# An fp32 attention product as three fp32r products, and the token mix shared between ScalarE and VectorE

## What is computed

```python
mod = (silu(c) @ wmod).reshape(8, 6, 1, -1)
sa, ca, ga, sb, cb, gb = (mod[:, n] for n in range(6))
ga = sign(ga) * maximum(abs(ga), 0.25)         # gb the same
h = layernorm(x) * (1 + ca) + sa
x = x + ga * attn(h)
h = layernorm(x) * (1 + cb) + sb
x = x + gb * ffn(h)

def attn(x):                       # 8 heads of 64; softmax over features, not tokens
    q, k, v = split(x @ w_qkv + b_qkv)
    scores = einsum('bhld,bhle->bhde', q, k) / sqrt(64)
    out = einsum('bhld,bhde->bhle', v, softmax(scores))
    return layernorm(out @ w_fc + b_fc + x) * gamma + beta

def ffn(x):
    prev = x shifted by one token (zeros first)
    xr = mu_r * x + (1 - mu_r) * prev
    xk = mu_k * x + (1 - mu_k) * prev
    r = sigmoid(xr @ W_r.T); k = xk @ W_k.T
    return r * (square(relu(k)) @ W_v.T)
```

## Time and profile before

| what | value |
|---|---|
| median of 3 runs | 691.06 us (689.15 to 691.09) |
| profiled execution, its own time | 690.6 us |
| its span, first to last instruction | 688.9 us |
| mean granted TensorE clock | 0.991 |
| TensorE matmuls, busy | 670.7 us, 97% |
| VectorE, busy | 561.0 us, 81% |
| ScalarE, busy | 393.8 us, 57% |
| GpSimd, busy | 317.5 us, 46% |

### The profile page before, as it was taken

The page is one execution under the profiler, slowest core; times in us unless marked ns, Lnnn a source line. Parts: engine busy times, 40 slices in busy tenths (PEclk is TensorE's granted clock), DMA queues, the critical chain, the costliest instruction groups (busy, mean ns, idle before and its releaser), DMA issues.

```text
span 688.9 us, 11754 instructions
## 1 busy us (share of the span) xinstructions
PE 670.7 (97%) x3712; PEld 539.4 (78%) x3712; DVE 561.0 (81%) x1254; ACT 393.8 (57%) x871; POOL 317.5 (46%) x520
## 2 busy tenths in 40 slices
PE   7988999999999999999999999999999999999896
PEld 6777886888778887879868887788878788687674
DVE  5693999789887998889887898979988898658973
ACT  1424575566754675474855667546754747547662
POOL 5272864573254642565335742646325753214320
PEclk9989999999999999999999999999999999999999
DMA  8849345485836666572855849366665528628225
GB/s 316 232 152 222 103 131 123 77 212 97 209 74 142 163 135 147 99 167 92 198 113 79 219 91 213 67 141 158 145 136 99 107 72 173 123 37 179 37 31 91
DMA packets 90984, 93.02 MB, mean 135 GB/s; under 512 B 4224, under 2 KB 89000, under 8 KB 90960
## 3 DMA queue, kind: packets, MB, share of 16 engines
q0 software_dynamic: 33264, 33.03, 32.6%
q1 hardware_dynamic: 55344, 55.97, 25.6%
q10 hardware_dynamic: 2352, 3.73, 1.5%
HBM read 42.84 MB, written 33.10 MB: 110 GB/s over the span
## 4 chain that ended last, share of the span: by engine, by line
PE 86%; DVE 7%; POOL 2%; DMA 2%; issue 1%; ACT 1%; SPq 0%; DVEq 0%; POOLq 0%
PE work L1335 14%; PE work L1318 14%; PE att L1285 13%; PE gram L1267 11%; PE gram L1398 4%; PE att L1370 4%; PE work L1151 4%; PE tr L1260 4%; PE work L1153 4%; PE work L1152 4%; PE tr L1302 4%; PE att L1389 2%; PE gram L1380 1%; PE att L1318 1%; DVE st L907 1%
## 5 line engine op out<-in xcount | busy, mean ns | idle before, releaser
L471 POOL TENSOR_TENSOR rs<-ve,neg_half 128x4 f32<-128x4 f32 x32 | 41.6, 1300 | 161.4 <-DVE ve L917 161.4
L1285 PE MATMUL att<-m_sb,z_t 128*128 128x256 f32 x496 | 112.4, 380 | 1.6 <-issue 0.8
L1335 PE MATMUL work<-mx,w_k_t 128*128 128x512 f32 x236 | 106.2, 592 | 0.0
L1285 PEld LDWEIGHTS att<-m_sb,z_t 128*128 128x128 f32 x496 | 92.4, 190 | 16.9 <-issue 5.7
L1318 PE MATMUL work<-w_r_t,mx 128*128 128x256 f32 x464 | 105.7, 381 | 0.0
L1318 PEld LDWEIGHTS work<-w_r_t,mx 128*128 128x128 f32 x464 | 85.9, 190 | 11.1
L1267 PE MATMUL gram<-z 128*128 128x256 f32 (+1 forms) x512 | 90.7, 331 | 0.0
L1267 PEld LDWEIGHTS gram<-z 128*128 128x128 f32 x512 | 81.1, 194 | 6.9
L934 DVE SCALAR_TENSOR_TENSOR mx<-t_buf,mu_col,h2t 128x512 f32<-128x512 f32 x120 | 84.3, 765 | 1.1
L654 ACT ACTIVATE sq<-att 128x256 f32<-128x256 f32 x124 | 46.1, 383 | 64.1 <-PE att L1285 64.1
L1335 PEld LDWEIGHTS work<-mx,w_k_t 128*128 128x128 f32 x236 | 44.8, 190 | 44.1 <-issue 42.6
(11 more groups left out here) (170 smaller groups left out, 1283.6 us busy)
## 6 DMA issues: line engine op xcount, KB each, us to landing
x_in<-in_L_attn_x_dram SPq DMA_DIRECT2D x32, 512.0 KB, 4.8
x<-rows SPq DMA_DIRECT2D x32, 512.0 KB, 3.4
x<-in_L_attn_x_dram POOLq DMA_DIRECT2D x32, 512.0 KB, 8.9
out_dram<-x SPq DMA_DIRECT2D x31, 512.0 KB, 5.1
out_dram<-y POOLq DMA_DIRECT2D x29, 512.0 KB, 6.2
rows<-row_scratch SPq DMA_DIRECT2D x16, 128.0 KB, 4.1
rows<-row_scratch SPq DMA_DIRECT2D x8, 256.0 KB, 3.8
wqkv_sb<-in_L_attn_w_qkv_dram ACTq DMA_DIRECT2D x1, 1536.0 KB, 9.7
```

The source lines that it names most:

```text
L1285: ins = mm(att_banks(j, alone)[q][:, (t % 2) * D:(t % 2 + 1) * D], z_t[:, j, k, t * P:(t + 1) * P], m_sb[:, k], start=(k == 0), stop=(k == ...
L1335: ins = mm(k_banks(alone)[dh][:], w_k_t[:, ch, rows_dh], mixed(j, alone)[1][:, ch], start=(ch == 0), stop=(ch == KD - 1))
```

## The change

Four things change together.

1. The attention product uses the same three-product form as the feed-forward output: z_t is replaced by z_hi (ScalarE's copy now rounds to fp32r) and z_lo (VectorE subtracts, low_z), and M by m_hi and m_lo (VectorE, two more instructions in make_m). The banks tr are free only when z_lo is made.
2. The mix of rows 0 to 6 has no difference any more. ScalarE writes mu times h2 (scale_r, scale_k: four activations per chunk), and VectorE adds (1 - mu) times the shifted h2 (mix_r, mix_k: four multiply-adds). The last row keeps the old form (mix_alone), but with the ordinary buffers.
3. k_hi and k_lo have one buffer in place of two; the last chunk of all uses z_hi.
4. Lists in another order, mostly around chunks 1 and 3; GpSimd's prep_wv stands later in the row; in the start, VectorE makes z_lo of row 0 and the column 1 - mu (make_rest), and ScalarE waits for the small loads.

```diff
@@ attention, TensorE
-                            ins = mm(att_banks(j, alone)[q][:, (t % 2) * D:(t % 2 + 1) * D], z_t[:, j, k, t * P:(t + 1) * P], m_sb[:, k],
-                                     start=(k == 0), stop=(k == KD - 1))
+                            ins = mm3(att_banks(j, alone)[q][:, (t % 2) * D:(t % 2 + 1) * D],
+                                      (z_hi[:, j, k, tile], z_lo[:, j, k, tile], m_hi[:, k], m_lo[:, k]),
+                                      start=(k == 0), stop=(k == KD - 1))
@@ turn_z2, TensorE
-                elif not last and j < CH - 1:
-                    pe.wait_ge(z_t_ready, 2 * (i + 1 + CH) + 2)
+                    if not last and j < CH - 1:
+                        pe.wait_ge(z_lo_ready, 2 * (i + 1 + CH) + 1 + h)
@@ ScalarE
+            def scale_r(b, j):
+                i = CH * b + j
+                wait_past(act, r_done, 2 * i - 2)
+                act.wait_ge(h2_ready, 2 * i + 2)
+                for h in range(KD):
+                    nc.scalar.activation(mixed(j)[0][:, h], h2t[:, h, 1 + j * CT:1 + (j + 1) * CT], ACT.Copy,
+                                         scale=mu_col[:, 0, h:h + 1]).then_inc(xr_scaled, 1)
...
@@ VectorE
+            def mix_r(b, j):
+                i, dst = CH * b + j, mixed(j)[0]
+                dve.wait_ge(xr_scaled, 2 * i + 2)
+                for h in range(KD):
+                    ins = nc.vector.scalar_tensor_tensor(dst[:, h], h2t[:, h, j * CT:(j + 1) * CT], rest_col[:, 0, h:h + 1],
+                                                         dst[:, h], ALU.mult, ALU.add)
+                ins.then_inc(xr_mixed, 1)
...
+            def low_z(b, j):
+                i = CH * b + j
+                for h in range(KD):
+                    dve.wait_ge(z_hi_ready, 2 * i + h + 1)
+                    nc.vector.tensor_tensor(z_lo[:, j, h], tr[h][:], z_hi[:, j, h].bitcast(F32),
+                                            ALU.subtract).then_inc(z_lo_ready, 1)
@@ make_m, VectorE
-                                        res[:].rearrange("p k d -> p (k d)"), ALU.add).then_inc(m_ready, 1)
+                                        res[:].rearrange("p k d -> p (k d)"), ALU.add).then_inc(m_step, 1)
+                dve.wait_ge(m_step, 2 * b + 1)
+                nc.vector.tensor_copy(m_hi[:], m_sb[:]).then_inc(m_step, 1)
+                dve.wait_ge(m_step, 2 * b + 2)
+                nc.vector.tensor_tensor(m_lo[:], m_sb[:], m_hi[:].bitcast(F32), ALU.subtract).then_inc(m_ready, 1)
@@ row_steps, ScalarE
                 copy_h2(b, 1)
+                make_z2(b, 2)
+                scale_r(b, 1)
+                copy_z_hi(n, 3)
                 squares(b, 3)
-                make_z2(b, 2)
-                copy_z_t(n, 3)
+                scale_k(b, 1)
                 copy_gram(n)
@@ start, VectorE
+            low_z(0, 2)
             rows_b()
+            low_z(0, 3)
             centre_fc()
+            make_rest()
             stats_a(1, 0)
```

More of the change, by code:

```diff
@@ L152, in adaln_block @@
         xr, xk = mx[:, 0], mx[:, 1]
-        k_hi, k_lo = (part(n, [P, 2, KD, CT]) for n in ("k_hi", "k_lo"))
+        k_hi, k_lo = (part(n, [P, KD, CT]) for n in ("k_hi", "k_lo"))
         y = sb("y", [P, 2, NT, D])
@@ L529, in row_steps @@
                 else:
-                    prep_wv(n)
                     rstd_o(b, 1)
@@ L917, in stats_2, with make_rest, mix_k, mix_alone @@
                 nc.vector.tensor_scalar(ve_2[:, s], ag_2[:, s, :, 1], EPS_LN, None, ALU.add).then_inc(ve_2_done, 1)
-            def mix(b, j, made=None, alone=False):
-                i = CH * b + j
[L922 to L927, removed]
+            def make_rest():
+                dve.wait_ge(small_loaded, 16 * 5)
+                nc.vector.tensor_scalar(rest_col[:], mu_col[:], -1.0, 1.0, ALU.mult, ALU.add).then_inc(rest_ready, 1)
+            def mix_r(b, j):
[5 more added lines that the diff above has]
+                ins.then_inc(xr_mixed, 1)
+            def mix_k(b, j):
+                i, dst = CH * b + j, mixed(j)[1]
+                dve.wait_ge(xk_scaled, 2 * i + 2)
+                for h in range(KD):
+                    ins = nc.vector.scalar_tensor_tensor(dst[:, h], h2t[:, h, j * CT:(j + 1) * CT], rest_col[:, 1, h:h + 1],
+                                                         dst[:, h], ALU.mult, ALU.add)
+                ins.then_inc(xk_mixed, 1)
+            def mix_alone(b, j, made):
+                i = CH * b + j
+                dve.wait_ge(r_done, 2 * i - 2)
+                dve.wait_ge(k_done, 2 * i - 2)
+                dve.wait_ge(xk_mixed, i)
+                dve.wait_ge(x2_ready, CH * b + made)
                 dve.wait_ge(h2_ready, 2 * i + 2)
@@ L930, in mix @@
                 nc.vector.tensor_tensor(dif, h2t[:, :, 1 + j * CT:1 + (j + 1) * CT], prev, ALU.subtract).then_inc(dif_done, 1)
-                dve.wait_ge(dif_done, i + 1)
-                for n, (dst, ready) in enumerate(zip(mixed(j, alone), (xr_mixed, xk_mixed))):
+                dve.wait_ge(dif_done, j + 1)
+                for n, (dst, ready) in enumerate(zip(mixed(j), (xr_mixed, xk_mixed))):
                     for h in range(KD):
@@ L1033, in row_steps @@
                 prep_now(n)
+                low_z(n, 0)
                 make_x2(b, 0)
@@ L1042, in row_steps @@
                 else:
+                    make_z(n, 2)
+                    low_k(b - 1, 3)
                     prep_qk(n)
-                    low_k(b - 1, 3)
-                    make_z(n, 2)
+                    low_z(n, 1)
                     make_x2(b, 1)
                     stats_2(b, 1)
-                mix(b, 0)
+                mix_r(b, 0)
+                mix_k(b, 0)
+                low_z(n, 2)
                 if first:
@@ L1057, in row_steps @@
                 make_z(n, 3)
-                mix(b, 1)
+                mix_r(b, 1)
+                low_z(n, 3)
                 gate_o(b, 0)
+                mix_k(b, 1)
                 make_x2(b, 3)
-                mix(b, 2)
+                mix_r(b, 2)
+                mix_k(b, 2)
                 low_k(b, 1)
@@ L1116, in _ @@
             make_z(0, 1, first=True)
+            low_z(0, 0)
             stats_a(0, 3)
@@ L1120, in _ @@
             prep_now(0)
+            low_z(0, 1)
             make_z(0, 3, first=True)
```

105 lines of the change are left out of this document (65 added, 40 removed).

## The result

The changed kernel takes 692.25 us (median of 15 runs, 690.96 to 695.2); the kernel before took 690.64 in the 15 runs beside it (688.79 to 692.7). The ratio is 1.0028, 95% interval 1.0015 to 1.0041: if anything slower, by 0.3%, which is less than the 2.1 us that the prediction took for the least that counts. Forecast were 680.6 and a range of 674 to 688, so the gain of 10 us did not come. The profiled execution took 692.31, with a span of 690.6 (before 690.6 and 688.9).

The account below looks back on a forecast made before the run. The prediction took TensorE's own work to bound the steady rows. Six steady rows at -13.7, row 0 +5.0 and last row -1.5 gave -10.2 from 690.6; time put at 680.6 us, 8-in-10 range 674 to 688.

Parts of the forecast that it names:

- part 4: GpSimd's moved wv step: make_z regains 2.5 us, the mix of chunk 2 loses 2.1, hidden by 2.6 of room.
- The third rival: Full block by GpSimd: mix of chunk 2 stopped 5.1 us, k_lo of chunk 1 2.5 late; 695.4 us, chance 0.06.
- the three signs of being wrong: Period above 78.6 or below 77.4; largest new steady-row TensorE wait elsewhere than forecast; row 0 under 3 us later.
- Part 1: Attention product on TensorE: 2.74 us instead of 3.45, saving 0.71 per chunk, 2.84 per row.
- Part 3: ScalarE's four scalings per chunk at 0.62 us each make TensorE wait 0.55 per row for the Gram copy.
- Part 2: VectorE's low z parts and M split, less the mix's difference: net +1.1 us per row, no steady-row cost from the split.
- The start and row 0: VectorE leads: 0.9 at the start, 1.15 for the M split, 2.4 added work, 0.55 Gram wait; 5.0 us later.
- The last stretch: Last row: no low_z but shorter attention products, half of the 2.84 let through, -1.5 us.

Follow-up runs that it names:

- b1: The kernel before with one edit, GpSimd's prep_wv moved to its new place, row 0 included: 703.59 us, ratio 1.0192.
- a2: The changed kernel with ScalarE's k scaling of chunk 1 moved behind the Gram copies: 730.27 us, ratio 1.0565.
- b2: The changed kernel with, in the loop's rows, prep_wv at its old place and VectorE's prep_qk behind make_z of chunk 3: 684.06 us, ratio 0.9897.
- c2: b2 with all three products of the attention product made from the high parts of z and M: 683.7 us, ratio 0.9896.
- b3: b2 with Gram copies ahead of chunk 3's squares and r of chunk 1 ahead of chunk 2's k scaling, row 0 too: 691.44 us, ratio 1.0014.
- c3: b2 with, in the loop's rows, Gram copies ahead of chunk 1's k scaling and r of chunk 1 ahead of chunk 2's: 684.9 us, ratio 0.9918.
- a1: The changed kernel with prep_wv back at its old place in the loop's rows: 690.53 us, ratio 0.9994.
- a4: The changed kernel with the edit of a2 and prep_wv one step earlier, where VectorE makes z of chunk 3: 706.35 us, ratio 1.0216.
- a3: The changed kernel with the edits of a1 and a2 together: 699.07 us, ratio 1.0112.
- b4: The changed kernel with its attention product in plain fp32, low part of z made but not used: 706.12 us, ratio 1.0207.
- c1: b2 with SyncE no longer waiting for M's low part before loading the next ca row: 683.51 us, ratio 0.9890.

## Why the prediction was wrong

**The step that failed is part 4, the sentence "between it and the k_lo of chunk 1 I count 2.6 us of room, so nothing shows".** The count of room was about right. The loss was not: I took 2.1 from row 0, and it is 4.25. Output 1 begins 2.0 late, so the room was 2.25 and not 2.6, and with the 0.32 that comes back in the product 1.68 per row is left. That is 10 us over six rows, most of the miss of 11.65. The trace of before held the answer. The mix of row 0, 95.81 to 100.65, met the first of GpSimd's two products, 97.40 to 100.10, and ended 0.55 after it; the second ran all but its first 0.47 beside VectorE instructions that read PSUM, which lost nothing. GpSimd's row, then VectorE's:

```profile
100.18 2.22 POOL L499 TENSOR_TENSOR wv_aug<-wv_aug 128x1020 f32<-128x1020 f32 x1
```

```profile
100.58 1.27 DVE L952 SCALAR_TENSOR_TENSOR y<-y,work 128x512 f32<-128x512 f32 x2
101.77 1.65 DVE L896 SCALAR_TENSOR_TENSOR t_buf<-att,rs_o,g_row 128x256 f32<-128x256 f32 x4
```

At the new place each of the two products meets a VectorE instruction with both inputs in SBUF. I read one meeting as the price of the step, when it was the price of one instruction. The third rival had the mechanism, at 0.06; its own price (5.1 lost, 2.5 late) was too high by 0.85 in the loss and 0.5 in the lateness, and what was blocked was the residual sum and half of the mix, not the mix alone. Two of the three signs of being wrong that the prediction names came: the period is above 78.6, and the largest new wait is not ScalarE's but the one before output 1.

b1 shows this piece alone, a2 shows the block at full length (7.00 for 1.41, one instruction held by each product), and b2 shows that with the meeting taken out of both places in the loop rows the kernel is 1.0% faster than before.

**Part 1.** The products save, but about 0.59 each, not 0.71: three of the four in a row take 2.86 to 2.96 from start to start and not the output product's 2.74. Four make -2.35 with their neighbours, not -2.84; 2.9 us over six rows. The row that I took for the price was the same form in another place, and c2 shows that the low parts are not the reason for the difference. Read from start to start, that same output product took 2.93 in the kernel before (288.61 to 291.54 in TensorE's timeline), so part of the 0.71 was in the reading.

**Part 3** was right: scalings of 0.62, no gap, a wait of 0.66 at the Gram transpose against 0.55. Another order of ScalarE's list, which I did not claim to help, didn't in b3 and c3.

**Part 2.** The M split costs nothing in a steady row; k_lo of chunk 0 and the turn of z2 hold. What I missed is that the new VectorE list leaves prep_wv's old place without cover as well (a1).

**The start and row 0.** Together +4.0 against +5.0, a near hit that is partly luck: the early part was taken too high, and 1.1 of row 0 comes from a wait that was not forecast. The start has +0 and not +0.9. From the mark to the output product of chunk 0, row 0 is 2.5 later (42.49 after the mark, before 39.99) and not 1.15 + 2.4 = 3.55, for the ca row came only 0.3 later after the mark (10.67 against 10.35), not 1.15. Then come the Gram transpose (+0.5) and output 1 (+1.1, with 0.91 of idle time), the block again.

**The last stretch.** -1.0 against -1.5.

With the two mis-sized terms put right my sum reads 680.6 + 10.0 + 2.9 = 693.5 against 692.25.

## What to carry to other kernels

When a GpSimd step is moved, price it instruction by instruction: for each of its large products, find which VectorE instruction on SBUF operands will stand beside it, and count that one as starting anew when GpSimd's ends. A slowed pair of rows seen elsewhere in the trace gives the price of that meeting only. Place such a step where VectorE is idle or reads PSUM. An instruction with one SBUF tensor is no safe neighbour: make_z was slowed from 1.37 to 3.89 in the kernel before and to 5.20 in a4. Putting GpSimd's step back and VectorE's prep_qk into a gap that VectorE already had (b2) turned 692 into 684.

## What the runs showed of the hardware that was not expected

- The block is nearly complete and counts as busy time: 1.23 us became 3.87 and 5.18, 1.41 became 3.03 and 7.00, and four instructions with one SBUF tensor went from 1.37 to 5.20 (a4).
- GpSimd loses too: its second product went from 1.89 to 2.76, and an instruction on 128x4 elements (0.20 alone) took 2.59 beside VectorE's mix in row 0 of b2, which kept its own 1.41 a pair. The first product, 3.44 against 2.41, doesn't show it: its record begins 1.03 before that of the DMA issue ahead of it ends, and it took 3.41 to 3.44 wherever that issue stood ahead of it.
- Twenty-four fp32r matmuls of one shape run at 120 ns each in the attention product and at 113 to 118 in the output product; the attention product keeps its 120 with the high parts alone (c2).
- Behind a wait of 5.2 us TensorE's granted clock was 0.50 for 2.6 us (a2), and the product there took 2.2 more. Behind the same 2.02 us of idle time in row 0 it stayed at 1.00 over the next 3.6 us in the profiles of eight kernels and was 0.53 to 0.63 in four (a1, a3, b4, c1).
